# Edge stage of a GNN + MoE kernel: static order of GpSimd's gathers and scatters, own index semaphores, zeroing from SyncE's queue

## The chip, the cores and the metric

The kernel runs on one core of a Trainium2 chip (trn2). The metric is the device time of one execution in microseconds.

## The reference

Nodes N = 50000 with D = 256 features, 25000 edges, 8 experts. Cut to what matters:

```python
# stage 1: edges.  H in f16, w = edge_weight in f16
msgs = layernorm(x).astype(f16)[dst] * w[:, None]
x = x + segment_sum(msgs, src, num_segments=50000)      # f16 sums
# stages 2 and 3: a layer norm, a top-1 router over 8 experts with capacity, two-layer experts
h = layernorm(x)
idx, p = argmax/prob of softmax(h @ gate_w + gate_b)
x = x + (relu(h @ w1[idx] + b1[idx]) @ w2[idx] + b2[idx]) * (p * kept)
```

The change touches stage 1 alone.

## The kernel before, in words

The program has three stages, each a block of five engine programs with a barrier behind it: the edge stage (`edge_and_constants`), the router (`route_tokens`) and the experts (`run_experts`). The router reads what the edge stage added up in a DRAM buffer `agg`, so it starts only when the edge stage has ended on every engine.

The edge stage works in steps of 1024 edges: 25 steps, numbered 0 to 24, the last one overlapping the one before it. In each step:

- SyncE (SP) loads `dst_col`, `src_col`, `w_col` and `src_row` (src repeated on 128 partitions), lines 159 to 163. They share one semaphore `idx_loaded[h]` for each of `INPUTS` = 3 buffers, and wait until the step that used the buffer is computed (`edge_done`, line 157).
- GpSimd (POOL) gathers the rows of x that `dst` names: eight indirect transfers of 128 rows, `gather`, lines 186 to 198. It waits for all four loads of the step and for a free buffer of `rows`.
- VectorE takes the statistics of the rows once all eight have landed (line 305), builds comparison masks (line 292), scales the messages (line 340), and writes the `target` rows (line 349), which increments `edge_done`.
- ScalarE takes the square root, normalises (line 265), and copies TensorE's sums from PSUM to `sums` in four parts (line 275, `sums_out`).
- TensorE counts, and adds up the messages with equal src inside the step by 64 matmuls with the masks (lines 365 to 376).
- GpSimd scatters the sums into `agg` by eight indirect transfers that add (`scatter`, lines 200 to 215). Scatter s waits for `edge_done` and `sums_out` of step s and until scatter s-1 has landed, since two adds to one row must not overlap. Scatter 0 also waits until `agg` is zeroed.

`agg` is zeroed by 25 transfers of 1 MB, which ScalarE issues between its instructions of the first steps (`zero`, line 246). `sums` and `target` have `HOLD` = 6 buffers. GpSimd's order is written out by hand: gathers of steps 0 to 5, then in turn scatter s and gather s+6 (eight calls each) as long as there are steps, with a hardware loop in the middle (lines 217 to 238). The other engines run steps in order, unrolled by `HOLD`, with the first `HOLD` steps outside of the loop.

Of the kernel before, what the change touches and what calls it, by code (L numbers as in the profile page):

```python
# [27 lines left out]
I32 = mybir.dt.int32  # L28
# [28 lines left out]
HOLD = 6  # L57
INPUTS = 3
# [14 lines left out]
def edge_and_constants(nc, ctx, t):  # L73
# [22 lines left out]
    dst_col = sb("dst_col", [P, INPUTS, G], I32)  # L96
# [27 lines left out]
    agg_zeroed = sem("agg_zeroed")  # L124
    idx_loaded = [sem(f"idx_loaded{r}") for r in range(INPUTS)]
# [16 lines left out]
    AHEAD = HOLD - 1  # L142
# [6 lines left out]
    with nc.Block() as block:  # L149

        @block.sync
        def _(sp):
            def load(i, r):
                s, h = HOLD * i + r, r % INPUTS

                if not (isinstance(i, int) and s < INPUTS):
                    sp.wait_ge(edge_done, s + 1 - INPUTS)
                b = base_of(i, r)
                sp.dma_start(dst_col[:, h, :], row_view(dst[bass.ds(b, STEP)])).then_inc(idx_loaded[h], 16)
# [3 lines left out]
                    .then_inc(idx_loaded[h], 16)  # L163
            steps(sp, S, HOLD, load)

# [9 lines left out]
        def _(pool):  # L175
# [10 lines left out]
            def gather(i, r):  # L186
                s, h = HOLD * i + r, r % INPUTS

                pool.wait_ge(idx_loaded[h], 64 * (turn(i, r) + 1))
                pool.nop(nofuse=True)  # L190
                if not (isinstance(i, int) and s < INPUTS):
                    pool.wait_ge(edge_done, s + 1 - INPUTS)
                    pool.nop(nofuse=True)
                for c in range(G):
                    pool.indirect_dma_start(
                        out=rows[:, h, c, :], out_offset=None, in_=x[:, :],
                        in_offset=bass.IndirectOffsetOnAxis(ap=dst_col[:, h, c:c + 1], axis=0),
                    ).then_inc(gathered[h], 16)

            def scatter(i, r):  # L200
                s = HOLD * i + r
# [4 lines left out]
                if isinstance(i, int) and s == 0:  # L206
                    pool.wait_ge(agg_zeroed, 16 * ZEROS)
                else:
                    pool.wait_ge(added[r - 1], 16 * G * (i + 1 if r else i))
                    pool.nop(nofuse=True)  # L210
# [6 lines left out]
            for r in range(AHEAD):  # L217
                gather(0, r)
            gather(0, AHEAD)
            scatter(0, 0)  # L220
            for r in range(1, HOLD):
                gather(1, r - 1)
# [1019 lines left out]
```

## Time and profile before

| | us |
|---|---|
| median of 3 runs | 3526.37 |
| lowest and highest run | 3525.03, 3540.87 |
| the profiled execution's own time | 3569.06 |
| its span | 3567.3 |
| GpSimd's last call of the edge stage starts | 703.73 |
| the router stage's first instruction on GpSimd | 713.84 |

The profile comes from one execution, taken by the hardware profiler. Start times in the timeline are microseconds from the span's start. An entry "[12.13 <-DMA src_row]" says that the engine was idle for 12.13 us before the instruction and what ended that. "issue" is time in which the engine waited for nothing that the profile shows. POOL is GpSimd, DVE VectorE, ACT ScalarE, PE TensorE, SP SyncE, and a name with a q behind it is the engine's DMA issuing.

### The profile page before, as it was taken

How to read it: one execution, taken by the hardware profiler on the slowest of the kernel's cores; microseconds unless marked ns; L12 is line 12 of the kernel's file. 1: busy time of each engine (PE TensorE's matmuls, PEld its weight loads, DVE VectorE, ACT ScalarE, POOL GpSimd, SP SyncE). 2: the span in 40 equal slices, each digit the busy share in tenths (PEclk: the TensorE clock that was granted, in tenths of full speed). 3: DMA queues.
4: the chain of work that ended last, by engine and by line, in shares of the span. 5: the costliest groups of instructions: out<-in, count | busy, mean ns of one | idle time of the engine just before them, and what ended most of it. 6: DMA issues, size and time to landing. Idle time of an engine off the chain costs nothing.

```text
span 3567.3 us, 60077 instructions
## 1 busy us (share of the span) xinstructions
PE 2846.6 (80%) x18806; PEld 2603.9 (73%) x18807; DVE 2245.0 (63%) x5836; ACT 1539.7 (43%) x2638; POOL 1724.4 (48%) x1183
## 2 busy tenths in 40 slices
PE   4553434067677777499999999999999999999998
PEld 3443433067676667399898999888999989998987
DVE  5645555076566566377666677676677776667666
ACT  2322222044444444255444555454455545554443
POOL 4788887635555566333434333343433343334323
PEclk8666666555555555699999999999999999999999
DMA  8544444388787776311211211121211121111111
GB/s 313 153 89 77 87 78 86 29 269 252 249 259 248 228 240 207 115 48 56 66 57 44 72 48 52 49 67 57 67 48 47 56 67 47 48 51 49 42 47 37
DMA packets 306007, 374.74 MB, mean 105 GB/s; under 512 B 34887, under 2 KB 266340, under 8 KB 302608
## 3 DMA queue, kind: packets, MB, share of 16 engines
q1 hardware_dynamic: 224608, 202.49, 19.3%
q0 software_dynamic: 77728, 145.22, 14.9%
q10 hardware_dynamic: 3600, 26.22, 1.8%
q8 instruction: 28, 0.46, 0.1%
q14 instruction: 43, 0.35, 0.0%
HBM read 185.42 MB, written 196.46 MB: 107 GB/s over the span
## 4 chain that ended last, share of the span: by engine, by line
PE 53%; DVE 4%; issue 1%; DVEq 0%; DMA 0%; SPq 0%; ACT 0%; POOL 0%; POOLq 0%; ACTq 0%
PE u_Y L1181 27%; PE u_H L1170 23%; PE u_T L1153 3%; DVE y L1110 1%; DVE yo L1129 1%; DVE yo L1126 1%; DVE y L1115 0%; DVE hn L1078 0%; DVE low L1120 0%; DVE hlo L1098 0%; DVE yo L1124 0%; DMA slots<-blank 0%; DMA u_pay<-slots 0%; DVE scales L1073 0%; DVEq L1078 0%
## 5 line engine op out<-in xcount | busy, mean ns | idle before, releaser
L1010 POOL DMA_INDIRECT out_x<-yo,u_token x348 | 668.5, 1921 | 1261.4 <-DVE yo L1131 1179.5
L1181 PE MATMUL u_Y<-whi,hhi 128*128 128x256 f32 x2784 | 784.2, 282 | 1.5 <-DVE hlo L1098 1.5
L1181 PE MATMUL u_Y<-wlo,hhi 128*128 128x256 f32 x2784 | 775.4, 279 | 0.0
L1181 PE MATMUL u_Y<-whi,hlo 128*128 128x256 f32 x2784 | 774.8, 278 | 0.0
L1046 ACT ACTIVATE hm<-u_H,b1e 128x512 f32<-128x512 f32 (+1 forms) x736 | 487.9, 663 | 639.8 <-PE u_H L1170 627.0
L539 POOL DMA_INDIRECT slots<-pay,slot_i x392 | 415.3, 1059 | 325.5 <-DVE slot_i L748 210.3
L1170 PE MATMUL u_H<-xhi,whi 128*128 128x512 f32 (+1 forms) x1472 | 563.6, 383 | 8.0 <-issue 5.5
L1170 PE MATMUL u_H<-xhi,wlo 128*128 128x512 f32 (+1 forms) x1472 | 562.2, 382 | 0.0
L1170 PE MATMUL u_H<-xlo,whi 128*128 128x512 f32 (+1 forms) x1472 | 560.2, 381 | 0.0
L1181 PEld LDWEIGHTS u_Y<-whi,hhi 128*128 128x128 f32 x2784 | 528.4, 190 | 1.7 <-DVE hlo L1098 1.7
L1181 PEld LDWEIGHTS u_Y<-wlo,hhi 128*128 128x128 f32 x2784 | 528.8, 190 | 0.0
L1181 PEld LDWEIGHTS u_Y<-whi,hlo 128*128 128x128 f32 x2784 | 528.1, 190 | 0.0
L1110 DVE TENSOR_TENSOR y<-u_Y,b2e 128x256 f32<-128x256 f32 x348 | 123.9, 418 | 555.2 <-PE u_Y L1181 555.2
L1050 ACT ACTIVATE hhi<-hm 128x512 fp32r<-128x512 f32 (+1 forms) x736 | 448.7, 610 | 23.3
L1098 DVE TENSOR_TENSOR hlo<-hm,hhi 128x512 fp32r<-128x512 f32 (+1 forms) x736 | 454.0, 692 | 2.9 <-ACT hhi L1050 2.9
L604 PEld LDWEIGHTS ps_L<-gw,hT 128*128 128x128 f32 x1568 | 350.3, 332 | 43.9 <-ACT hT L566 26.5
L604 PE MATMUL ps_L<-gw,hT 128*128 128x8 f32 x1568 | 344.0, 353 | 39.8 <-ACT hT L566 24.5
L212 POOL DMA_INDIRECT agg<-sums,target x200 | 329.5, 1648 | 83.7 <-issue 58.8
L1170 PEld LDWEIGHTS u_H<-xhi,whi 128*128 128x128 f32 x1472 | 277.0, 188 | 64.8 <-issue 9.8
L1170 PEld LDWEIGHTS u_H<-xlo,whi 128*128 128x128 f32 x1472 | 277.2, 188 | 53.8
L1170 PEld LDWEIGHTS u_H<-xhi,wlo 128*128 128x128 f32 x1472 | 277.4, 188 | 50.4
L619 PE MATMUL ps_T<-ident,h 128*128 128x128 f32 x784 | 206.9, 430 | 115.0 <-ACT h L570 111.8
(137 smaller groups left out, 3747.9 us busy)
## 6 DMA issues: line engine op xcount, KB each, us to landing
xt<-in_x SPq DMA_DIRECT2D x49, 1024.0 KB
out_x<-pay SPq DMA_DIRECT2D x49, 1024.0 KB
u_pay<-slots SPq DMA_DIRECT2D x93, 534.0 KB, 3.8
agg<-zeros ACTq DMA_DIRECT2D x25, 1024.0 KB
at<-agg SPq DMA_DIRECT2D x49, 512.0 KB
raw<-in_L_ffn_w POOLq DMA_DIRECT2D x14, 1024.0 KB
src_row<-in_src SPq DMA_DIRECT2D x25, 512.0 KB
slots<-blank SPq DMA_DIRECT2D x8, 801.0 KB, 5.1
```

What stands on the lines that cost most here:

```text
L212: pool.indirect_dma_start(out=agg[:, :], out_offset=bass.IndirectOffsetOnAxis(ap=target[:, r, c:c + 1], axis=0), in_=sums[:, r, c, :], in_ ...
L539: pool.indirect_dma_start(out=slots[:, :], out_offset=bass.IndirectOffsetOnAxis(ap=slot_i[:, r, g:g + 1], axis=0), in_=pay[:, r, g, :], in ...
L604: last = pe.matmul(logits[:, g, :], hT[:, g * KD + kd, :], gw[:, kd, :], start=(kd == 0), stop=(kd == KD - 1))
L619: last = pe.transpose(ps_T[:, n, :], h[:, q, g, kd * P:(kd + 1) * P], ident[:])
L1010: pool.indirect_dma_start(out=out[:, :], out_offset=bass.IndirectOffsetOnAxis(ap=token[:, s:s + 1], axis=0), in_=yo[:, s, :], in_offset=No ...
L1046: act.activation(hm[:, f, cols], ps_H[:, f % 2, cols], ACT.Relu, bias=b1e[:, f:f + 1])\
L1050: act.activation(hhi[:, f, cols], hm[:, f, cols], ACT.Copy).then_inc(hhi_ready, 1)
L1098: v.tensor_tensor(hlo[:, f, cols], hm[:, f, cols], hhi[:, f, cols].bitcast(F32), ALU.subtract)\
L1110: last = v.tensor_tensor(y[:, s, :], ps_Y[:, s, 0:D], b2e[:], ALU.add)
L1153: last = pe.transpose(ps_T[:, k, s * P:(s + 1) * P], hn[:, s, k * P:(k + 1) * P], ident[:])
L1170: last = pe.matmul(ps_H[:, f % 2, cols], w1_at(w, buf, k, f), a[:, k, cols], start=(j == 0), stop=(j == len(passes) - 1))
L1181: last = pe.matmul(ps_Y[:, s, 0:D], a[:, f, rows], w2_at(w, buf, f), start=(f == 0 and j == 0), stop=(f == KF - 1 and j == 2))
```

## The change

- `HOLD` goes from 6 to 8, so `sums`, `target` and now `dst_col` have eight buffers; `INPUTS` from 3 to 4, so `rows`, `src_row`, `src_col` and `w_col` have four.
- `dst_col` gets semaphores of its own (`dst_loaded`). GpSimd waits for that load alone, VectorE for the other three. The load of `dst_col` is issued ahead of the wait for a free input buffer. The gather still waits until the step four before it is computed.
- The zeroing transfers move from ScalarE's to SyncE's queue: 13 behind the loads of step 3, and three each behind those of steps 4 to 7.
- GpSimd's program is static, without a hardware loop: all 64 gather calls of steps 0 to 7, scatter 0, and then the other 136 gather calls spread evenly, five or six of them ahead of each of the scatters 1 to 24.

```diff
--- before.py
+++ after.py
@@ -54,8 +54,8 @@
         return self.base + self.n
 
 
-HOLD = 6
-INPUTS = 3
+HOLD = 8
+INPUTS = 4
 
 
 def steps(eng, total, unroll, body):
@@ -93,7 +93,7 @@
     zeros = sb("zeros16", [P, 16 * D], F16)
     src_row = sb("src_row", [P, INPUTS, STEP], I32)
     src_col = sb("src_col", [P, INPUTS, G], I32)
-    dst_col = sb("dst_col", [P, INPUTS, G], I32)
+    dst_col = sb("dst_col", [P, HOLD, G], I32)
     w_col = sb("w_col", [P, INPUTS, G], F32)
     w16 = sb("w16", [P, 2, G], F16)
     w32 = sb("w32", [P, 2, G], F32)
@@ -122,6 +122,7 @@
     set_up = sem("set_up")
     pool_set = sem("pool_set")
     agg_zeroed = sem("agg_zeroed")
+    dst_loaded = [sem(f"dst_loaded{r}") for r in range(HOLD)]
     idx_loaded = [sem(f"idx_loaded{r}") for r in range(INPUTS)]
     gathered = [sem(f"gathered{r}") for r in range(INPUTS)]
     added = [sem(f"added{r}") for r in range(HOLD)]
@@ -139,7 +140,6 @@
 
     BANKS = G * D // 512
     PER_BANK = G // BANKS
-    AHEAD = HOLD - 1
     turn = lambda i, r: (HOLD // INPUTS) * i + r // INPUTS
     row_view = lambda ap: ap.rearrange("(p c) -> p c", c=G)
     agg_v = agg.rearrange("(p b r) d -> b p (r d)", p=P, r=16)
@@ -150,18 +150,32 @@
 
         @block.sync
         def _(sp):
+            def zero(count):
+                for _ in range(count):
+                    b = next(parts, None)
+                    if b is not None:
+                        sp.dma_start(agg_v[b], zeros[:]).then_inc(agg_zeroed, 16)
+
             def load(i, r):
                 s, h = HOLD * i + r, r % INPUTS
-
+                b = base_of(i, r)
+
+                sp.dma_start(dst_col[:, r, :], row_view(dst[bass.ds(b, STEP)])).then_inc(dst_loaded[r], 16)
                 if not (isinstance(i, int) and s < INPUTS):
                     sp.wait_ge(edge_done, s + 1 - INPUTS)
-                b = base_of(i, r)
-                sp.dma_start(dst_col[:, h, :], row_view(dst[bass.ds(b, STEP)])).then_inc(idx_loaded[h], 16)
                 sp.dma_start(src_col[:, h, :], row_view(src[bass.ds(b, STEP)])).then_inc(idx_loaded[h], 16)
                 sp.dma_start(w_col[:, h, :], row_view(weight[bass.ds(b, STEP)])).then_inc(idx_loaded[h], 16)
                 sp.dma_start(src_row[:, h, :], src[bass.ds(b, STEP)].partition_broadcast(P))\
                     .then_inc(idx_loaded[h], 16)
+                if isinstance(i, int) and i == 0 and r >= INPUTS - 1:
+
+                    if r == INPUTS - 1:
+                        sp.wait_ge(set_up, 1)
+                    zero(ZEROS - (HOLD - INPUTS) * 3 if r == INPUTS - 1 else 3)
+
+            parts = iter(range(ZEROS))
             steps(sp, S, HOLD, load)
+            assert next(parts, None) is None
 
             w1, w2, raw = t["w1"], t["w2"], t["raw"]
             WF = raw.shape[1] // 2
@@ -183,30 +197,30 @@
             pool.affine_select(out=ident[:], in_=ident[:], compare_op=ALU.not_equal, fill=1.0, base=0,
                                pattern=[[-1, P]], channel_multiplier=1).then_inc(pool_set, 1)
 
-            def gather(i, r):
-                s, h = HOLD * i + r, r % INPUTS
-
-                pool.wait_ge(idx_loaded[h], 64 * (turn(i, r) + 1))
-                pool.nop(nofuse=True)
-                if not (isinstance(i, int) and s < INPUTS):
-                    pool.wait_ge(edge_done, s + 1 - INPUTS)
+            def gather(s, c):
+                r, h = s % HOLD, s % INPUTS
+                if c == 0:
+                    pool.wait_ge(dst_loaded[r], 16 * (s // HOLD + 1))
                     pool.nop(nofuse=True)
-                for c in range(G):
-                    pool.indirect_dma_start(
-                        out=rows[:, h, c, :], out_offset=None, in_=x[:, :],
-                        in_offset=bass.IndirectOffsetOnAxis(ap=dst_col[:, h, c:c + 1], axis=0),
-                    ).then_inc(gathered[h], 16)
-
-            def scatter(i, r):
-                s = HOLD * i + r
+                    if s >= INPUTS:
+
+                        pool.wait_ge(edge_done, s + 1 - INPUTS)
+                        pool.nop(nofuse=True)
+                pool.indirect_dma_start(
+                    out=rows[:, h, c, :], out_offset=None, in_=x[:, :],
+                    in_offset=bass.IndirectOffsetOnAxis(ap=dst_col[:, r, c:c + 1], axis=0),
+                ).then_inc(gathered[h], 16)
+
+            def scatter(s):
+                r = s % HOLD
 
                 pool.wait_ge(edge_done, s + 1)
                 pool.wait_ge(sums_out, BANKS * (s + 1))
                 pool.nop(nofuse=True)
-                if isinstance(i, int) and s == 0:
+                if s == 0:
                     pool.wait_ge(agg_zeroed, 16 * ZEROS)
                 else:
-                    pool.wait_ge(added[r - 1], 16 * G * (i + 1 if r else i))
+                    pool.wait_ge(added[(s - 1) % HOLD], 16 * G * ((s - 1) // HOLD + 1))
                     pool.nop(nofuse=True)
                 for c in range(G):
                     pool.indirect_dma_start(
@@ -214,49 +228,28 @@
                         in_=sums[:, r, c, :], in_offset=None, compute_op=ALU.add,
                     ).then_inc(added[r], 16)
 
-            for r in range(AHEAD):
-                gather(0, r)
-            gather(0, AHEAD)
-            scatter(0, 0)
-            for r in range(1, HOLD):
-                gather(1, r - 1)
-                scatter(0, r)
-            with pool.Fori(1, S // HOLD - 1) as i:
-                gather(i, AHEAD)
-                scatter(i, 0)
-                for r in range(1, HOLD):
-                    gather(i + 1, r - 1)
-                    scatter(i, r)
-            n = S // HOLD - 1
-            gather(n, AHEAD)
-            scatter(n, 0)
-            gather(n + 1, 0)
-            for r in range(1, HOLD):
-                scatter(n, r)
-            scatter(n + 1, 0)
+            HEAD = HOLD * G
+            SPREAD = S * G - HEAD
+            for n in range(HEAD):
+                gather(n // G, n % G)
+            scatter(0)
+            for s in range(1, S):
+
+                for n in range(HEAD + SPREAD * (s - 1) // (S - 1), HEAD + SPREAD * s // (S - 1)):
+                    gather(n // G, n % G)
+                scatter(s)
             for r in range(HOLD):
-                pool.wait_ge(added[r], 16 * G * (n + (2 if r == 0 else 1)))
+                pool.wait_ge(added[r], 16 * G * (S // HOLD + (r < S % HOLD)))
 
         @block.scalar
         def _(act):
 
             act.wait_ge(set_up, 2)
-            parts = iter(range(ZEROS))
-
-            def zero(i, count=1):
-                for _ in range(count if isinstance(i, int) and i == 0 else 0):
-                    b = next(parts, None)
-                    if b is not None:
-                        act.dma_start(agg_v[b], zeros[:]).then_inc(agg_zeroed, 16)
-
-            zero(0, 2 + max(0, ZEROS - AHEAD * (BANKS + 2)))
 
             def body(i, r):
                 s, h, q = HOLD * i + r, r % 2, r % INPUTS
-                zero(i)
                 act.wait_ge(stats_ready, s + 1)
                 act.activation(std[:, h, :], mv[:, h, :, 1], ACT.Sqrt, bias=eps[:, 0:1]).then_inc(std_ready, 1)
-                zero(i)
 
                 act.wait_ge(scale_ready, s + 1)
                 if not (isinstance(i, int) and s < 2):
@@ -269,12 +262,10 @@
                 if not (isinstance(i, int) and i == 0):
                     act.wait_ge(added[r], 16 * G * i)
                 for b in range(BANKS):
-                    zero(i)
                     act.wait_ge(summed, BANKS * s + b + 1)
                     part = slice(b * PER_BANK, (b + 1) * PER_BANK)
                     act.activation(sums[:, r, part, :], ps_sum[:, part, :], ACT.Copy).then_inc(sums_out, 1)
             steps(act, S, HOLD, body)
-            assert next(parts, None) is None
 
         @block.vector
         def _(v):
@@ -296,7 +287,7 @@
             def body(i, r):
                 s, h, q = HOLD * i + r, r % 2, r % INPUTS
                 n = Count(s * PER + SET)
-                v.wait_ge(idx_loaded[q], 64 * (turn(i, r) + 1))
+                v.wait_ge(idx_loaded[q], 48 * (turn(i, r) + 1))
                 v.tensor_copy(srcf[:, h, :], src_col[:, q, :])
                 v.tensor_copy(w16[:, h, :], w_col[:, q, :]).then_inc(step, n.inc())
 
```

Two places show how instructions move. The first is GpSimd at the end of the edge stage. `rows<-in_x,dst_col` is a gather call, `agg<-sums,target` a scatter call; eight of either make a step. Before, the rows begin with the gather of step 23:

```order
L195 DMA rows<-in_x,dst_col 128x256 [waits idx_loaded2,edge_done]
L195 DMA rows<-in_x,dst_col 128x256 x7
L212 DMA agg<-sums,target 51200x256 [waits edge_done,sums_out,added5]
L212 DMA agg<-sums,target 51200x256 x7
L195 DMA rows<-in_x,dst_col 128x256 [waits idx_loaded0,edge_done]
L195 DMA rows<-in_x,dst_col 128x256 x7
L212 DMA agg<-sums,target 51200x256 [waits edge_done,sums_out,added0]
L212 DMA agg<-sums,target 51200x256 x7
L212 DMA agg<-sums,target 51200x256 [waits edge_done,sums_out,added1]
L212 DMA agg<-sums,target 51200x256 x7
L212 DMA agg<-sums,target 51200x256 [waits edge_done,sums_out,added2]
L212 DMA agg<-sums,target 51200x256 x7
```

In the kernel before, scatters 19 to 24 all follow the last gather; three of them are shown. After the change, the last twelve rows of the stage:

```order
L209 DMA rows<-in_x,dst_col 128x256 [waits dst_loaded7,edge_done]
L209 DMA rows<-in_x,dst_col 128x256 x3
L226 DMA agg<-sums,target 51200x256 [waits edge_done,sums_out,added5]
L226 DMA agg<-sums,target 51200x256 x7
L209 DMA rows<-in_x,dst_col 128x256 x4
L209 DMA rows<-in_x,dst_col 128x256 [waits dst_loaded0,edge_done]
L209 DMA rows<-in_x,dst_col 128x256
L226 DMA agg<-sums,target 51200x256 [waits edge_done,sums_out,added6]
L226 DMA agg<-sums,target 51200x256 x7
L209 DMA rows<-in_x,dst_col 128x256 x6
L226 DMA agg<-sums,target 51200x256 [waits edge_done,sums_out,added7]
L226 DMA agg<-sums,target 51200x256 x7
```

The gather call that waits for `dst_loaded7` is the first of step 23, the one that waits for `dst_loaded0` the first of step 24. The scatter behind `added5` is step 22, behind `added6` step 23, behind `added7` step 24. The last gather calls now stand just ahead of the last scatters.

The second place is the zeroing. Before, on ScalarE, at the start of the stage:

```order
L250 DMA agg<-zeros 128x4096 [waits set_up]
L250 DMA agg<-zeros 128x4096 x2
L258 ACT_TABLE_LOAD
L258 ACTIVATE e_std<-e_mv,eps 128x8 [waits e_stats_ready]
L250 DMA agg<-zeros 128x4096
L265 ACTIVATE norm<-rows,e_offset,e_rstd 128x256 [waits scale_ready]
L265 ACTIVATE norm<-rows,e_offset,e_rstd 128x256 x7
L250 DMA agg<-zeros 128x4096
L275 ACTIVATE sums<-ps_sum 128x512 [waits summed]
L250 DMA agg<-zeros 128x4096
L275 ACTIVATE sums<-ps_sum 128x512 [waits summed]
```

After the change, on SyncE, from the loads of step 3 to those of step 4:

```order
L163 DMA dst_col<-in_dst 128x8
L166 DMA src_col<-in_src 128x8
L167 DMA w_col<-in_edge_weight 128x8
L168 DMA src_row<-in_src 128x1024
L157 DMA agg<-zeros 128x4096 [waits set_up]
L157 DMA agg<-zeros 128x4096 x12
L163 DMA dst_col<-in_dst 128x8
L166 DMA src_col<-in_src 128x8 [waits edge_done]
L167 DMA w_col<-in_edge_weight 128x8
L168 DMA src_row<-in_src 128x1024
L157 DMA agg<-zeros 128x4096 x3
```

ScalarE issues no transfers any more, and SyncE has the 13 transfers between the loads of step 3 and `dst_col` of step 4.

## Rows read from the trace of the kernel before

**Rows 1.** The page, busy tenths of 40 slices of 89 us, and a DMA issue line.
```profile
POOL 4788887635555566333434333343433343334323
...
DMA  8544444388787776311211211121211121111111
...
agg<-zeros ACTq DMA_DIRECT2D x25, 1024.0 KB
```

**Rows 2.** Windows: us, busy PE, PEld, DVE, ACT, POOL, then PEclk, DMA share, GB/s.
```profile
50.00:60.00 10.00, 5.20 (x52) 4.48 (x53) 6.35 (x21) 4.04 (x8) 7.12 (x8) 0.54 1.01 418
254.00:274.00 20.00, 10.55 (x100) 9.69 (x100) 7.33 (x34) 2.11 (x4) 16.04 (x14) 0.76 0.48 99
```

**Rows 3.** Groups by line, 0 to 900 us, GpSimd's two calls.
```profile
L212 POOL DMA_INDIRECT agg<-sums,target x200 | 329.5, 1648 | 83.7 <-issue 58.8 <-DMA agg<-sums,target 12.6 <-DMA agg<-zeros 12.0
...
L195 POOL DMA_INDIRECT rows<-in_x,dst_col x200 | 194.3, 971 | 95.7 <-issue 61.9 <-DMA src_row<-in_src 33.5 <-DMA agg<-sums,target 0.3
```

**Rows 4.** Timeline of GpSimd, head: start us, duration us, instruction, [idle before].
```profile
7.94 1.14 POOL L195 DMA_INDIRECT rows<-in_x,dst_col  x1 [5.86 <-DMA src_row<-in_src]
...
16.91 0.95 POOL L195 DMA_INDIRECT rows<-in_x,dst_col  x1 [0.30 <-issue]
...
50.75 1.05 POOL L195 DMA_INDIRECT rows<-in_x,dst_col  x1 [12.13 <-DMA src_row<-in_src]
...
76.14 0.94 POOL L195 DMA_INDIRECT rows<-in_x,dst_col  x1 [15.53 <-DMA src_row<-in_src]
...
88.67 0.95 POOL L195 DMA_INDIRECT rows<-in_x,dst_col  x1 [2.46 <-issue]
...
111.31 1.63 POOL L212 DMA_INDIRECT agg<-sums,target  x1 [11.96 <-DMA agg<-zeros]
```

**Rows 5.** Timeline of GpSimd, the end of the stage.
```profile
603.34 0.94 POOL L195 DMA_INDIRECT rows<-in_x,dst_col  x1 [0.30 <-issue]
...
622.65 1.54 POOL L212 DMA_INDIRECT agg<-sums,target  x1 [2.54 <-DMA agg<-sums,target]
...
703.73 1.55 POOL L212 DMA_INDIRECT agg<-sums,target  x1 [0.30 <-issue]
713.84 0.13 POOL L525 IOTA token_i<- 128x8 int32 x1 [8.57 <-POOLq L149]
```

**Rows 6.** Timeline of ScalarE's queue, zeroing transfers.
```profile
3.27 2.17 ACTq L250 DMA_DIRECT2D agg<-zeros  x3
...
103.20 0.34 ACTq L250 DMA_DIRECT2D agg<-zeros  x1
```

**Rows 7.** Timeline of SyncE's queue, loads of steps 0, 3 and 4.
```profile
0.96 0.41 SPq L159 DMA_DIRECT2D dst_col<-in_dst  x1
...
41.74 0.33 SPq L159 DMA_DIRECT2D dst_col<-in_dst  x1
...
62.54 0.33 SPq L159 DMA_DIRECT2D dst_col<-in_dst  x1
```

**Rows 8.** Timeline of VectorE, head: statistics of step 0, targets of steps 0 and 3.
```profile
20.33 2.71 DVE L305 BATCH_NORM_STATS2 e_stats<-rows 128x6 f32<-128x256 f32 x8 [13.00 <-DMA rows<-in_x,dst_col]
...
41.55 0.17 DVE L349 TENSOR_TENSOR target<-shift,srcf 128x8 int32<-128x8 f32 x1
...
100.52 0.17 DVE L349 TENSOR_TENSOR target<-shift,srcf 128x8 int32<-128x8 f32 x1
```

**Rows 9.** Timeline of VectorE and ScalarE, step 24.
```profile
606.06 2.71 DVE L305 BATCH_NORM_STATS2 e_stats<-rows 128x6 f32<-128x256 f32 x8 [10.57 <-DMA rows<-in_x,dst_col]
...
620.92 0.17 DVE L349 TENSOR_TENSOR target<-shift,srcf 128x8 int32<-128x8 f32 x1
...
629.54 0.60 ACT L275 ACTIVATE sums<-ps_sum 128x512 f16<-128x512 f32 x1 [1.15 <-PE ps_sum L376]
```

**Rows 10.** Timeline of VectorE and ScalarE, step 10.
```profile
242.56 2.71 DVE L305 BATCH_NORM_STATS2 e_stats<-rows 128x6 f32<-128x256 f32 x8 [11.60 <-DMA rows<-in_x,dst_col]
...
273.68 0.60 ACT L275 ACTIVATE sums<-ps_sum 128x512 f16<-128x512 f32 x1 [5.90 <-remote]
```

## The prediction

> **What bounds the kernel now.** The page first: GpSimd (POOL) is the busiest engine of the first seventh of the span, at 7 to 8 tenths, and the DMA row falls from 8 tenths to 4 after the first slices [rows 1]. A stretch from the middle, 254 to 274 us, shows why nothing else bounds it: GpSimd is busy 16.0 of 20 us and in issue gaps for the rest, TensorE 10.6, VectorE 7.3, DMA at 0.48 [rows 2]. The groups by line over the first 900 us give the price of GpSimd's calls: 200 scatters of 1648 ns and 200 gathers of 971 ns, each with 0.30 us of issue ahead of it (58.8 and 61.9 us over some 195 calls) [rows 3]. So a gather call is 1.27 us, a scatter call 1.95 us, a step of eight and eight 25.8 us, and 25 steps 254 + 390 = 644 us.
>
> GpSimd's timeline gives the rest. The first gather starts at 7.9. Then come three waits for a step's index loads (12.1 and 15.5 us, and 2.5 at step 5), and one of 12.0 us for the zeroing of agg [rows 4]; at the end, where no gathers are left between scatters, five waits of 2.5 us for the scatter before to land [rows 5]. Check: 7.9 + 644 + (12.1 + 15.5 + 2.5 + 12.0 + 5 x 2.5 less 0.3 each in the issue already counted, 52) = 704; the last call ends at 703.73 + 1.55 = 705.3 [rows 5]. The next stage opens 8.6 us later and depends on that. A microsecond of the edge stage is a microsecond of the kernel.
>
> **Zeroing off ScalarE's queue.** The 25 issues cost ScalarE nothing it lacks (its copies wait for TensorE), so removing them: 0. What counts is when the 25 transfers of 1 MB land [rows 1].
>
> **The start.** GpSimd now waits for dst_col alone, not for src_row. The landing it waited for came at 7.9; dst_col is issued at 0.96 [rows 7], so the first gather comes about 4 us earlier. That gain reaches the end only if nothing waits behind it, and something does: rows has four buffers, so the gather of step g still waits for step g-4 to be computed. "Eight ahead" is eight gathered before the first scatter, not eight ahead of the computing. The first scatter (call its start T0) must wait for gather 7, which waits for the end of step 3. In the trace steps 0 and 3 end at 41.7 and 100.7 (DVE's target) [rows 8], about 20 us a step, against 10.2 us that eight gathers need. The computing sets the head, and I leave its pace as it is.
>
> Then gather 7 ends at 100.7 + 10.2 = 110.9. The last three zeroing transfers are issued behind the same end of step 3 and three loads, about 3 us after it; the last one before took 8.1 us from issue (103.2) to the scatter it released (111.3) [rows 4, 6]: 112. So T0 does not come earlier than the 111.3 of now, though 64 gathers stand before it and not 48. 13 of the zeroing transfers now come in one burst near 8 us (16 loads at 0.41 us and a little between them, from 0.96 [rows 7]). I add 3 us for it (bounds: 9 us below, if a head without scattered zeroing computes faster, to 15 above, the flood below). **T0 = 115.**
>
> **The middle.** After T0: 136 gathers x 1.27 = 172.7 and 200 scatters x 1.95 = 390.0. The 2.5 us landing waits go, covered by five or six gathers (6.3 us or more). Scatter calls are 1.54 us when VectorE is idle and 1.65 in the mean [rows 3, 5]; before, 160 of them lay beside VectorE's work of 20 steps, 21 us in all; now three of these steps are computed while GpSimd waits: -3 us. Steps 8 to 19 are gathered well ahead of their scatters: the last call of step 19 is followed by a whole scatter batch more than the next ones. Middle: 560 us.
>
> **The end, where the change pays.** The 136 calls are spread evenly over 24 gaps. The order shows what this does: the last call of step 24 is the call just before scatter 24; step 23's last call has two gathers behind it and then scatter 23; step 22's has four. A step needs all its eight calls before its statistics begin. Step 24 of the trace is such a step, computed with no gathers beside it: its last gather call ends at 604.28, the statistics start at 606.06, the target is written at 621.1, the last copy of its sums ends at 630.14 [rows 5, 9]: 25.9 us from the last gather to the release of its scatter. Before, this was hidden by five scatter batches. Now it is not:
> - scatter 24: 25.9 us of waiting,
> - scatter 23: 25.9 - 2 x 1.27 = 23.4,
> - scatter 22: 25.9 - 4 x 1.27 = 20.8,
> - scatters 21 and 20: steps whose last call is followed by one and three gathers, a scatter batch (15.6) and six gathers (7.6), so 24.5 and 27.0 us of cover. With gathers beside the copies a step takes longer: the one that starts its statistics at 242.56 ends its copies at 274.28, 31.7 us, against 24.1 in step 24 [rows 9, 10]. Between 1.4 us together and 11; I take 5.5.
>
> Sum of the waits: 75.6 us. The scatters form a chain, so each wait moves all that follows, and gathering and computing cannot run on meanwhile, since GpSimd issues both.
>
> **The sum**, in the profiled execution (span 3567.3, time 3569.06): GpSimd's last call ends at 115 + 560 + 75.6 = 750.6 against 705.3: **+45 us**. The profiled execution stands 43 us above the median of the three runs, 3526.37 (the highest of them is 3540.87); I take the difference over unchanged: 3526.4 + 45 = **3571 us**, 1.3% slower.
>
> **A page against the rows.** Index loads issued beside the zeroing took long: step 3's were issued from 41.7 and released GpSimd at 50.75, step 4's 62.5 and 76.1 [rows 4, 7]. They were on SP's queue while the zeroing was on ScalarE's. The Trainium skill, "DMA: Bandwidth & Descriptors", section "Queues, rings and completion order", says that SP and ACT own one ring each on the same 16 DMA engines, that an engine takes whole packets from the rings in turn, and consumes one ring in order. By that rule dst_col of step 4, now issued behind 13 transfers on one ring, waits for all of them, and each gather call waits for a packet of zeroing. The trace agrees that loads suffer; that they stand in line, no row here shows. My sum has 3 us for this, by that rule it has up to 15.
>
> **The rivals.**
> - *The flood sets the head.* One zeroing transfer is 1 MB, 64 KB per DMA engine, at the 418 GB/s of 50 to 60 us [rows 2] 2.5 us; a gather call is 128 KB, 0.3 us. If they alternate, a step's rows need 8 x 2.8 = 22 us to land and not 10. Step 0 is half issued before the burst and loses some 5 us, step 1 a few more. Step 4's indices come at 8.5 us + 13.6 MB / (418 less the gathers' 105 GB/s) = 52 us, and not at step 0's end at 42, which costs nothing, since gather 7 waits for step 3 anyway. If TensorE's first steps slow too, T0 is 130: +60, 3586 us. For it: DMA at 1.00 wherever zeroing runs. Against: step 0's last call ended at 17.9 and its statistics began at 20.3, 2.5 us later, with three such transfers issued ahead of it [rows 4, 6, 8].
> - *The waits at the end are halved.* If a step alone needs less than the trace's 25.9 us (VectorE has no earlier step to finish, TensorE no copies to wait for) the waits shrink threefold with each microsecond; at 15 us they are 15 + 12.5 + 9.9 = 37, the end is 115 + 560 + 37 = 712, +7: within 0.5%, 3533 us.
> - *The other side: no waits at the end.* The one mechanism is the cover. If spreading the calls kept computing ahead of scattering to the end, GpSimd would run without a pause, and the end would be 115 + 560 = 675: -30, 3496 us. It decides at a latency of 7.6 us (six gathers) for step 24 and less for the others. The start of the stage speaks for it, where three steps of gathers are in hand; step 24's 25.9 us [rows 9], of which the 9.0 us from the target to the last copy alone are more than the cover, speak against it.
> - *The change does nothing*: the head bound by computing, the end as before. But then scatter 24 would need its rows long before, and the order says otherwise.
>
> **How the numbers follow.** Forecast (three full waits, T0 106 to 122): 0.76. Flood on top: 0.11. Halved waits: 0.09. No waits: 0.04. Half a percent, 17.6 us, is about what a measurement of this kernel can tell from no change. Slower by more: forecast, flood and a little of the halved case, 0.88; within: 0.08; faster: 0.04. Range: below, T0 at 106, waits of 70 and scatters 10 us cheaper give +21; I go to +20, 3546. Above, the flood with 11 us at scatters 20 and 21 gives +66, 3592.
>
> **What the changed profile would show.** First gather near 4; step 3's end near 100; first scatter at 112 to 118, released by the zeroing or by the last gather's end; no waits for agg to land; then on GpSimd three waits of 20 to 26 us for ScalarE's copies before the last three scatter batches, and the last call near 750. TensorE's share in the later stages is unchanged. I am wrong if these three waits sum to under 50 us, or if T0 lies below 100 or over 130.

## The result and the profile after

The changed kernel takes 3586.96 us (median of four runs, 3579.25 to 3590.17). The kernel before takes 3533.62 us in four runs, the three of the table above among them. The ratio is 1.0148, 95% interval 1.0113 to 1.0184, and the medians lie 53 us apart, where 45 were forecast. 3586.96 lies inside the range of 3546 to 3592, 16 us above the 3571 that was said.

The page of the changed kernel, GpSimd and DMA in tenths of the 40 slices:

```profile
POOL 5688887426666666433433433343433343334323
...
DMA  8544444148888786321211211121211121111111
```

GpSimd is as busy as before up to the seventh slice and falls to 4 in the eighth (628 to 718 us), where it showed 6 [rows 1]; the router stage, visible as DMA at 8, fills the tenth slice and only half of the ninth. The waits of the edge stage, for GpSimd alone (engine, line, waited for: total us, times, longest):

```profile
POOL agg L226 <- ACT sums L267: 70.6, 3, 26.2
POOL rows L209 <- issue: 62.5, 196, 3.1
POOL agg L226 <- issue: 61.9, 193, 3.2
...
POOL rows L209 <- DVE target L340: 15.2, 2, 10.9
POOL rows L209 <- DMA dst_col<-in_dst: 14.5, 2, 13.1
...
POOL agg L226 <- DMA dst_col<-in_dst: 6.6, 1, 6.6
```

The first line is new: three waits of GpSimd for ScalarE's copies, 70.6 us. The landing waits (a scatter waiting until the scatter before it has landed in `agg`) are gone. A scatter waits for several semaphores, and the trace names one of them: scatter 0 does not wait for `dst_col` at all, and the 6.6 us in the last line are read here as its wait for the zeroing, which e2 below names at the same place. The groups of the two calls, against [rows 3]:

```profile
L226 POOL DMA_INDIRECT agg<-sums,target x200 | 324.3, 1621 | 140.0 <-ACT sums L267 70.6 <-issue 61.9 <-DMA dst_col<-in_dst 6.6
L209 POOL DMA_INDIRECT rows<-in_x,dst_col x200 | 197.2, 986 | 92.2 <-issue 62.5 <-DVE target L340 15.2 <-DMA dst_col<-in_dst 14.5
```

The calls cost nearly what they did, 27 ns less for a scatter, 15 ns more for a gather. GpSimd's timeline at the head, against [rows 4]:

```profile
3.53 1.14 POOL L209 DMA_INDIRECT rows<-in_x,dst_col  x1 [1.42 <-DMA dst_col<-in_dst]
...
57.39 0.95 POOL L209 DMA_INDIRECT rows<-in_x,dst_col  x1 [13.09 <-DMA dst_col<-in_dst]
...
106.37 0.94 POOL L209 DMA_INDIRECT rows<-in_x,dst_col  x1 [10.89 <-DVE target L340]
...
123.11 1.78 POOL L226 DMA_INDIRECT agg<-sums,target  x1 [6.64 <-DMA dst_col<-in_dst]
```

The gathers start 4.4 us earlier, gather 4 waits for its indices until 57, gather 7 for the end of step 3 until 106, and the first scatter comes at 123.1 (111.3 before). At the end, against [rows 5]:

```profile
605.29 1.61 POOL L226 DMA_INDIRECT agg<-sums,target  x1 [3.18 <-issue]
...
646.45 1.62 POOL L226 DMA_INDIRECT agg<-sums,target  x1 [20.24 <-ACT sums L267]
...
692.83 1.62 POOL L226 DMA_INDIRECT agg<-sums,target  x1 [24.14 <-ACT sums L267]
...
714.08 0.95 POOL L209 DMA_INDIRECT rows<-in_x,dst_col  x1 [0.30 <-issue]
...
741.24 1.61 POOL L226 DMA_INDIRECT agg<-sums,target  x1 [26.20 <-ACT sums L267]
...
754.28 1.54 POOL L226 DMA_INDIRECT agg<-sums,target  x1 [0.30 <-issue]
765.48 0.14 POOL L516 IOTA token_i<- 128x8 int32 x1 [9.66 <-POOLq L149]
```

These are scatters 21, 22, 23 and 24. Between the last gather call (714.08) and scatter 24 (741.24) stands step 24, alone:

```profile
716.82 2.71 DVE L296 BATCH_NORM_STATS2 e_stats<-rows 128x6 f32<-128x256 f32 x8 [34.56 <-DMA rows<-in_x,dst_col]
...
730.83 0.17 DVE L340 TENSOR_TENSOR target<-shift,srcf 128x8 int32<-128x8 f32 x1
...
739.78 0.60 ACT L267 ACTIVATE sums<-ps_sum 128x512 f16<-128x512 f32 x1 [1.15 <-PE ps_sum L367]
```

From the end of the last gather call, 715.03, to the end of the last copy, 740.38, is 25.3 us, against 25.9 in [rows 9]; the scatter starts 0.9 us after it. The last call ends at 755.8, 50.5 us later than before. The two profiled spans differ by 21 us only (3588.4 and 3567.3), since the router stage, from its first instruction on GpSimd to its last scatter call, took 741 us in the profiled execution before and 707 in this one. The first run below asks whether that is the change.

### The profile page after: what moved, and what is told of

Same layout as the page of the kernel before. It is cut to its first block, busy times and chain, and to the rows that moved or that the text cites. A ratio compares the mean times of both kernels' runs of the same rounds, so it can differ in the third digit from the quotient of the medians.

```text
span 3588.4 us, 59975 instructions
## 1 busy us (share of the span) xinstructions
PE 2837.7 (79%) x18806; PEld 2604.7 (73%) x18807; DVE 2245.5 (63%) x5836; ACT 1544.4 (43%) x2638; POOL 1733.7 (48%) x1183
## 4 chain that ended last, share of the span: by engine, by line
PE 53%; DVE 4%; issue 1%; DVEq 0%; DMA 0%; SPq 0%; ACT 0%; POOL 0%; POOLq 0%; ACTq 0%
PE u_Y L1172 27%; PE u_H L1161 24%; PE u_T L1144 3%; DVE y L1101 1%; DVE yo L1120 1%; DVE yo L1117 1%; DVE y L1106 0%; DVE hn L1069 0%; DVE low L1111 0%; DVE hlo L1089 0%; DVE yo L1115 0%; DMA slots<-blank 0%; DMA u_pay<-slots 0%; DVE scales L1064 0%; DVEq L1069 0%
## 5 line engine op out<-in xcount | busy, mean ns | idle before, releaser
L530 POOL DMA_INDIRECT slots<-pay,slot_i x392 | 424.9, 1084 | 282.3 <-DVE slot_i L739 166.7
L226 POOL DMA_INDIRECT agg<-sums,target x200 | 324.3, 1621 | 140.0 <-ACT sums L267 70.6
L357 PE MATMUL ps_cnt<-ones,earlier 128*128 128x1 f16 x200 | 31.4, 169 | 451.9 <-DVE earlier L325 405.0
L357 PEld LDWEIGHTS ps_cnt<-ones,earlier 128*128 128x128 f16 x200 | 25.2, 132 | 457.1 <-DVE earlier L325 410.4
```

The lines of the kernel that those rows point to most:

```text
L226: pool.indirect_dma_start(out=agg[:, :], out_offset=bass.IndirectOffsetOnAxis(ap=target[:, r, c:c + 1], axis=0), in_=sums[:, r, c, :], in_ ...
L357: last = pe.matmul(ps_cnt[:, c:c + 1], earlier[:, h, c, :], ones[:, 0:1], start=(c == 0), stop=True)
L530: pool.indirect_dma_start(out=slots[:, :], out_offset=bass.IndirectOffsetOnAxis(ap=slot_i[:, r, g:g + 1], axis=0), in_=pay[:, r, g, :], in ...
```

## Experiments

Each kernel ran beside the kernel before, on the same chip. Three chips were used, on which the kernel before takes 3567, 3441 and 3565 us; which chip the first comparison (3534 us) ran on is not on record. "First scatter" and "end" are the start of the first and the end of the last scatter call, in us of the profiled execution. "N gaps" says how many of the gaps between scatters got gather calls; the changed kernel has 24.

| run | ratio to before (95%) | first scatter | end |
|---|---|---|---|
| the changed kernel | 1.0148 (1.0113 to 1.0184) | 123.1 | 755.8 |
| e1, before again | one run, no ratio | 112.9 | 707.2 |
| e2, 22 gaps | 0.9944 (0.9929 to 0.9960) | 121.0 | 688.6 |
| e3, whole steps | 0.9984 (0.9971 to 0.9998) | 123.1 | 701.3 |
| e4, zeroing on ScalarE | 1.0160 (1.0141 to 1.0179) | 125.8 | 761.7 |
| b2, before, gather 24 late | 1.0076 (1.0062 to 1.0089) | 106.0 | 720.6 |
| b3, 22 gaps, seven steps ahead | 0.9941 (0.9928 to 0.9955) | 97.9 | 676.8 |
| e5, gather 3 held back | 1.0113 (1.0097 to 1.0128) | 104.8 | 739.4 |
| b4, b3 and e5 | 0.9934 (0.9920 to 0.9947) | 98.5 | 677.3 |
| c1, the changed kernel again | 1.0152 (1.0137 to 1.0168) | 124.4 | 757.7 |
| c2, 23 gaps | 0.9970 (0.9952 to 0.9988) | 124.2 | 698.5 |
| c3, b3 again | 0.9967 (0.9954 to 0.9980) | 112.4 | 690.7 |
| c4, six and three buffers, 22 gaps | 0.9951 (0.9934 to 0.9968) | 101.9 | 691.2 |

e1 to e4 ran on one chip, b2 to b4 and e5 on the second, c1 to c4 on the third.

**The kernel before again (e1).** No edit.

> The kernel before, unchanged, for a second profile. Theory A (the edge stage alone moved; the 21 us between the two profiled spans and the 53 us between the medians differ because the router stage of the first profile happened to be long, 741 us from its first instruction to its last scatter against 707 in the changed kernel): the edge stage again ends at 705 +- 3 us, the router stage takes 705 to 725, and the span is 3525 to 3545. Rival B (the changed edge stage makes the router stage 33 us shorter): the router stage again takes about 741 and the span is about 3567.

The edge stage ends at 707.2, as expected, the router stage takes 728 us and the span is 3555.7. For the router and the span neither theory's number came (705 to 725 or 741, and 3525 to 3545 or 3567). But in all profiled executions on this chip and the third, whichever kernel, the router stage takes 728 to 736, and on the second chip 616 to 619. So it goes with the chip and not with the edge stage, and Rival B is out. Why the first two profiles show 741 and 707 stays open: their chips are not on record. The edge stage's own 50 us is what the medians show.

**The end: 22 gaps (e2).**

```diff
-                for n in range(HEAD + SPREAD * (s - 1) // (S - 1), HEAD + SPREAD * s // (S - 1)):
+                for n in range(HEAD + SPREAD * min(s - 1, 22) // 22, HEAD + SPREAD * min(s, 22) // 22):
```

> The changed kernel with its 136 spread gather calls in the first 22 gaps and not in all 24, so that the last two scatters have no gathers ahead of them. Theory A (the three waits of 20, 24 and 26 us for step 22, 23 and 24 are the loss): they go, two landing waits of 2.2 us come, the first scatter stays near 123, the last call ends at 755.8 - 70.6 - 3 + 4.4 = 687 and the kernel is some 68 us faster than the changed one, 3519, about 15 us faster than before. Rival B (computing has become the bound of the last steps, as its steps come late): the waits move ahead to other scatters and less than half of the 70 us comes back, 3555 or more.

The end comes at 688.6, 687 was expected, and the kernel is 0.56% faster than before. GpSimd's idle times over 2 us from the first scatter on:

```profile
121.00 1.63 POOL L226 DMA_INDIRECT agg<-sums,target  x1 [4.89 <-DMA agg<-zeros]
```

```profile
657.24 1.54 POOL L226 DMA_INDIRECT agg<-sums,target  x1 [2.56 <-DMA agg<-sums,target]
...
674.16 1.54 POOL L226 DMA_INDIRECT agg<-sums,target  x1 [2.46 <-DMA agg<-sums,target]
```

All three waits for copies are gone, and nothing took their place but two landing waits. This one line of the change is the loss; the rest of it was worth a little.

How much, and by what, can be added up against e1, the kernel before on the same chip, which ends at 707.2. The first scatter comes 8.1 us later (121.0 for 112.9); 16 gather calls of 1.27 us more have been made by then, so 20.3 us fewer are left behind it; and two landing waits of 2.2 us stand where e1 has five, 6.6 us less. That gives 18.8 us, and 18.6 were measured.

**One gap fewer (c2).** The same edit with 23 for 22, on the third chip.

> The changed kernel with its 136 spread calls in 23 gaps: the last gather stands ahead of scatter 23, so one scatter batch covers step 24. Theory A (a wait is the latency of 25.5 us less what GpSimd issues after the step's last gather): one wait of 25.5 - 14.6 - 0.3 = 10.6 us ahead of scatter 24, at most 1 us ahead of scatter 23 (2 gathers, a scatter batch, 6 gathers: 25.2 us of cover), none ahead of 22; the last call 60 us before that of the changed kernel. Rival B (the steps at the end wait for each other on VectorE and ScalarE): waits of over 5 us ahead of scatters 22 and 23 stay.

```profile
660.28 1.62 POOL L226 DMA_INDIRECT agg<-sums,target  x1 [2.79 <-issue]
...
683.99 1.54 POOL L226 DMA_INDIRECT agg<-sums,target  x1 [8.36 <-issue]
```

Ahead of scatter 24 GpSimd waits 8.4 us (10.6 expected), ahead of 23 2.8 (up to 1), and the end is 59.2 us before that of c1 (60 expected). The two misses are one: step 23, with gather calls beside it, takes 25.9 us from its statistics to its last copy where step 24 takes 23.9, and what GpSimd waits ahead of scatter 23 covers step 24 as calls would. The trace names no cause for either wait ("issue"); that scatter 24 starts at 683.99, 0.8 us after the last copy ends at 683.18, shows what it waited for. With the waits of the changed kernel (20, 24 and 26 us at 24 gaps) and none at 22 the rule "latency less cover" holds within 2.2 us at four lengths of cover.

**The cause put into the kernel before (b2).**

```diff
-            gather(n + 1, 0)
             for r in range(1, HOLD):
                 scatter(n, r)
+            gather(n + 1, 0)
             scatter(n + 1, 0)
```

> The kernel before with one batch moved: the gather of step 24 stands between scatters 23 and 24 and not ahead of scatter 19. Theory A (a gather just ahead of its scatter exposes the step's whole latency, 25.9 us): GpSimd waits 25 to 26 us for ScalarE's copies ahead of scatter 24, scatter 19 gets a landing wait of 2.2 us and scatter 24 loses one; the last call ends at 706 + 26 = 732, ratio to before 1.007. Rival B (computing alone, with no gathers beside it and the clock up, is much shorter than the trace's step 24): the wait is 15 us or less, ratio 1.004 or less.

```profile
679.21 0.95 POOL L195 DMA_INDIRECT rows<-in_x,dst_col  x1 [0.30 <-issue]
...
705.96 1.62 POOL L212 DMA_INDIRECT agg<-sums,target  x1 [25.80 <-ACT sums L275]
```

One batch moved costs 25.8 us of waiting and 0.76% of 3441 us, 26 us. The end, 720.6, is not the 732 that was expected: on this chip the first scatter comes at 106.0 and not at 111.3, and the calls cost less. The wait and the ratio came as Theory A had them. So the late gather makes the wait, shown in both directions.

**Whole steps (e3).** As e2 with 17 for 22: eight calls ahead of scatters 1 to 17.

> The changed kernel with eight gather calls ahead of each of the scatters 1 to 17 and none later, as the kernel before orders them, but with eight steps ahead. Theory A (only the end's cover counts): seven bare scatters cost 7 landing waits of 2.2 us, 15 in all; the last call ends near 687 + 11 = 698, the kernel about 3530, level with before. Rival B (even spreading itself makes scatter and gather calls cheaper or the computing faster): 10 us or more worse than that, 3540 or more.

The end is 701.3 (698 expected), 12.7 us after e2's; seven landing waits of 2.2 us against two are 11 of it. The first scatter comes 2.1 us later as well. So spreading to scatter 22 is worth what the landing waits cost.

**The zeroing back on ScalarE (e4).** Three transfers at the start, then one between ScalarE's instructions, as before; all else as changed.

```diff
+            zero(0, 2)
...
+                zero(i)
                 act.wait_ge(stats_ready, s + 1)
```

> The changed kernel with the zeroing transfers back on ScalarE's queue, between its instructions as before; the late waits stay. Theory A (the burst of 13 transfers slows step 0, whose target came at 49.1 and not 41.7, and the index loads behind it): step 0's target comes at 42 again, step 3's at 100, the first scatter at 111 to 114 and not 123, the last call at 745, the kernel 8 to 12 us faster than the changed one, 3576. Rival B (the first scatter comes late because it stands behind 64 gathers, wherever the zeroing is issued): first scatter at 120 or later, kernel within 4 us of the changed one, 3587.

My expectation was wrong, and the numbers of Rival B came. Step 0's target comes at 49.0 again, the first scatter at 125.8, and the ratio is 1.016 where the changed kernel has 1.015. The burst is not what slows step 0. VectorE's target of step 0 in e4:

```profile
48.82 0.17 DVE L339 TENSOR_TENSOR target<-shift,srcf 128x8 int32<-128x8 f32 x1
```

What these kernels share is that GpSimd, with four row buffers, issues gather calls until 44 us, where three buffers stopped it at 38.6 and step 0 was done at 41.7. That gave a new theory: gather calls beside a step hold it up. Rival B's reason, the 64 gathers ahead, fits too for the first scatter, but says nothing of step 0.

**Gather 3 held back until step 0 is computed (e5), and the same on b3 (b4).**

```diff
-                    if s >= INPUTS:
+                    if s >= INPUTS - 1:
 
-                        pool.wait_ge(edge_done, s + 1 - INPUTS)
+                        pool.wait_ge(edge_done, max(1, s + 1 - INPUTS))
```

> The changed kernel with one wait more: gather 3 starts only when step 0 is computed, as with three input buffers. Theory A (gather calls beside a step hold up TensorE's counts and the copies: step 0's target came at 42 before and at 49 with gathers issued until 44, wherever the zeroing is issued): step 0's target comes at 41 to 43, step 3's at 98 to 101, the first scatter at 114 to 118 instead of 123, and the kernel is 5 to 8 us faster than the changed one, ratio to before 1.013. Rival B (DMA at full load from the burst of zeroing is what holds up step 0): its target still comes at 47 to 49 and nothing is gained.

> b3 with the pause of e5. Theory A: first scatter 5 to 7 us before b3's, last call near 672, ratio to before 0.990. Rival B (the pause moves step 0's end only, and the zeroing sets the first scatter): within 2 us of b3.

This told nothing of the theory, since the runs fell on the second chip: step 0's target comes at 34.0 with the pause (e5) and at 34.6 without (b3), where gathers run until 45. From its statistics to its target step 0 takes 14 us there in either, and 14.0 in b2; before, it took 21.4 [rows 8]. None of the times expected for e5 fits that chip, and b4 ends within 0.5 us of b3, as its Rival B had it. e5 still has its three waits at the end, 20.7, 24.4 and 26.3 us, so the loss is there on the second chip too. Its ratio, 0.9934, is the best one measured, but its interval overlaps b3's.

**Seven steps ahead and the zeroing one load earlier (b3, again as c3).** With e2's gaps:

```diff
-            HEAD = HOLD * G
+            HEAD = (HOLD - 1) * G
...
-                    zero(ZEROS - (HOLD - INPUTS) * 3 if r == INPUTS - 1 else 3)
+                    zero(ZEROS - 9 if r == INPUTS - 1 else 3)
```

> The kernel with 22 gaps (e2) and, besides, seven steps gathered ahead of the first scatter and not eight, and the zeroing issued one load earlier (16, 3, 3, 3 behind the loads of steps 3 to 6). Theory A (the first scatter waits for the end of step 3 through gather 7 and the last zeroing): its time falls from 121 to about 100, the eight calls of step 7 follow later (10 us), the last call ends near 678 and not 688.6, the kernel is about 10 us faster than e2, ratio to before 0.9915. Rival B (what GpSimd gains at the first scatter it waits out later, since computing sets the pace until step 8): the last call ends within 3 us of e2's.

> b3 again (22 gaps, seven steps ahead, zeroing one load earlier), beside the changed kernel on one chip. Theory A: ratio to before 0.991 to 0.995; against the changed kernel 75 to 80 us less in the last call. Rival B (its gain came from one chip's fast first steps): where the first steps are slow the first scatter comes at 110 or later and the ratio is 0.997 or more.

On the second chip the first scatter comes at 97.9, as expected, but the kernel before gains there too (its first scatter, in b2, is at 106.0), and the ratio is 0.9941, not 0.9915. On the third the first scatter comes at 112.4 and the ratio is 0.9967, near Rival B's numbers; the last call comes 67 us before that of the changed kernel on this chip, and 75 to 80 were expected. The end, 690.7, is no earlier than e2's 688.6, since the eight calls that were not made ahead are made later: what an earlier first scatter gains, fewer calls ahead of it give back.

**The changed kernel again (c1).** No edit.

> The changed kernel again, on one chip with the next three. Theory A (the end waits are the loss on every chip, the start's part depends on how fast the chip computes the first steps): waits of 20, 24 and 26 us ahead of scatters 22 to 24; ratio to before 1.011 to 1.017. Rival B (the loss of the first comparison was of one chip): ratio under 1.008.

Waits of 20.8, 22.8 and 25.5 us, ratio 1.0152: the first comparison repeats on a chip where the kernel before takes 3565 us.

**Six and three buffers (c4).** e2's gaps, with the buffers of the kernel before:

```diff
-HOLD = 8
-INPUTS = 4
+HOLD = 6
+INPUTS = 3
```

> The changed kernel with HOLD = 6 and INPUTS = 3, as many buffers as before, and 22 gaps: static order and own index semaphores alone, six steps ahead. Theory A (more buffers bring nothing, the order does): first scatter at 97 to 105, no waits for computing at the end, last call within 4 us of b3's, ratio to before 0.991 to 0.995. Rival B (three row buffers stall the spread gathers): GpSimd waits for VectorE's target between scatters, last call 10 us or more later than b3's.

The end is 691.2 against 690.7 of c3 on the same chip, and the ratio 0.9951, at the edge of what was expected. So the added buffers bring nothing that shows. Where its gain over the kernel before comes from can again be added up, against e1 (on another chip; no profile of the kernel before was taken on this one): the same 48 calls are made ahead, the first scatter comes 11.0 us earlier (101.9 for 112.9), and three landing waits fewer are worth 6.6 us; 17.6 us in all, and the ends differ by 16.0. The larger part is the earlier first scatter: the last zeroing transfers are issued at 86.9 from SyncE's queue, where e1 issues its last one at 105.2 between ScalarE's instructions. No run moved the zeroing alone with six and three buffers.

c4 also bears on what e5 left open. On one chip, target of step 0, first c1 (four row buffers, gathers until 44.6), then c4 (three, gather 3 waits for this step, so the calls stop at 34.2):

```profile
49.34 0.17 DVE L340 TENSOR_TENSOR target<-shift,srcf 128x8 int32<-128x8 f32 x1
```

```profile
39.20 0.17 DVE L340 TENSOR_TENSOR target<-shift,srcf 128x8 int32<-128x8 f32 x1
```

10 us earlier, though 16 zeroing transfers and not 13 are issued in the burst beside it. The other reading would be that DMA at full load holds the step up. The stretch from 36 to 44 us, first of e4 (gather calls going on, the zeroing spread out), then of c4 (no gather calls, the burst), speaks against it (columns: busy PE, PEld, DVE, ACT, POOL, granted clock, DMA share, GB/s):

```profile
36.00:44.00 8.00, 1.96 (x36) 1.87 (x34) 0.35 (x2) 0.00 (x0) 6.17 (x7) 1.00 0.37 107
```

```profile
36.00:44.00 8.00, 7.18 (x64) 6.25 (x65) 5.72 (x27) 0.60 (x1) 0.00 (x0) 1.00 1.02 426
```

At a DMA share of 0.37 TensorE is busy for 2.0 of 8 us beside the gather calls, and at 1.02 for 7.2 us without them; the granted clock is 1.00 in both. In the changed kernel TensorE's adding up of step 0 starts at 48.44, after 6.96 us idle, and the gather calls had ended at 44.30; in the kernel before the two times are 41.15 (where it runs on without gaps) and 38.62. That speaks for the gather calls and against the zeroing. How they hold up the other engines is not shown, and an edit of nothing but the gather's wait on such a chip was not run.

## Why the prediction was right, and where it was off

- **The waits at the end.** Forecast: 25.9, 23.4, 20.8 us, and 5.5 for scatters 20 and 21, 75.6 in all. Measured: 26.2, 24.1, 20.2, and 3.0 (0.46 and 3.18, less the usual issue gap), 72.7 with the gaps taken off. The mechanism and the places were right, and so were the sizes of the three large waits. For scatters 20 and 21 the low end of "1.4 to 11" was the better one; where the 11 came from the prediction does not say. e2, c2 and b2 show the cause by taking it away, by giving part of the cover back, and by putting it in elsewhere.
- **The first scatter.** 115 was said, 106 to 122 allowed, and 123.1 came: the one clear error. The sum was 112 for the last zeroing (issued about 3 us after step 3, then 8.1 us) and 3 for the burst. Two of its terms were off. Step 3 ended at 105.6 and not at 100.7, so the last three transfers were issued at 108.0, 4.3 us later than 103.7. Here "the computing sets the head, and I leave its pace as it is" did not hold, since four row buffers let gather calls run on beside step 0, and on these chips that goes with a later step 0 (49.1 for 41.7). And from that issue to the first scatter it took 15.1 us and not 8.1, 7.0 us more. The 8.1 us were read from a single transfer, while three are issued together here; c1, e2, c2, c3 and c4, which issue three as well, show 13.6 to 14.9 us. 4.3 and 7.0, less the 3 allowed for the burst, are 8.3 us, against the 8.1 by which the sum was off. By e4 those 3 us had the wrong reason.
- **The middle.** 560 us was said, and 755.8 - 123.1 - 72.7 = 560.0. That it fits so closely is luck: scatters came 27 ns cheaper, 5.4 us in all where 3 were allowed, and gathers 15 ns dearer, 2 us.
- **The sum.** The edge stage came out +50.5 for +45, the medians +53 for +45. The 8.1 us of the first scatter, less the 2.9 that the waits came out shorter, are the 5.2 of the edge stage; in part the two errors cancelled.
- **Carrying it over to the median.** I took the profiled execution's +43 us over the median as a constant. It was not one: the changed kernel's profiled execution lies within 4 us of its median. 34 of the 43 us lie in the router stage, 741 us against 707. 3569 us is what a chip like those of e1 and c1 gives for the kernel before (3567 and 3565), so the profile may have come from another chip than the three runs; the record does not say. It did no harm to the forecast difference.
- **The page's rule.** dst_col of step 4 was issued at 27.35 behind the 13 transfers and released GpSimd at 57.39; 52 was worked out. By the Trainium skill, "DMA: Bandwidth & Descriptors", section "Queues, rings and completion order", one ring is consumed in order, and the trace agrees: the wait of 13.1 us at gather 4 names this load. In e4, with the zeroing on ScalarE's queue, gather 4 starts at 49.8, as soon as step 0 is computed (49.0). The late load cost the changed kernel nothing, as was said, because gather 7 waits for step 3 anyway.
- **The rivals.** The flood (T0 at 130) did not come in full, but it was nearer than the forecast's words suggest. At a DMA share of 1.02 from 12 to 50 us step 0's rows were used at 19.8, 6.4 us after its last gather call had ended (13.46), where before it was 2.5 us. So all but 0.5 of the 4.4 us by which the gathers started earlier were lost; the rival had said "some 5 us" for step 0. The burst on SyncE's queue is not needed for that: e4, with three transfers ahead, has 20.46 after 13.45. The halved waits fell with the 25.3 us of step 24. The kernel without waits fell with it too; its threshold of 7.6 us was misread, since no call at all stands between the last gather and scatter 24.

## What to carry to other kernels

Where one in-order engine issues both the inputs and the outputs of a pipeline, price the end of its order by itself: the wait ahead of the last output is the latency of a step less what the engine issues between that step's last input and its output. Spreading input calls evenly to the last output empties the pipeline just there; ending the spread two outputs early turned +1.5% into -0.6%. More lead at the start is worth the calls that it moves out of the busy stretch, less what it delays the first output: here 20.3 less 8.1 us in e2, and no more than six buffers brought in c4.

## What the runs showed of the hardware

**The chips differ in how soon an engine goes on after another.** In the profiled execution before, ScalarE's copies waited 213.9 us in the edge stage for something that the trace calls "remote", with the matmuls that they depend on recorded as ended; on the second chip (b2) no such wait stands in the list. In e1, on a chip where the kernel before takes 3567 us, it is 233.9 us. The waits of the kernel before:

```profile
ACT sums L275 <- remote: 213.9, 39, 12.2
DVE shift L343 <- remote: 23.6, 5, 8.0
```

In the kernel before, once the scatters have begun, a step beside gather calls takes 30 to 33 us from its statistics to its last copy (before and e1; [rows 10] is one), and 24.1 in step 24, which has none beside it. On the second chip (b2) every such step takes 23 to 24 us, with gather calls or without. The router stage shows it too. From 800 to 1300 us of the kernel before (e1) and of b2, whose router stage is the same (columns as above):

```profile
800.00:1300.00 500.00, 374.77 (x1970) 356.11 (x1970) 310.82 (x1246) 226.35 (x448) 297.91 (x276) 0.50 0.81 251
```

```profile
800.00:1300.00 500.00, 442.35 (x2364) 426.26 (x2364) 369.37 (x1482) 273.63 (x541) 387.67 (x332) 0.50 0.96 299
```

The granted clock is 0.50 in both (1.2 GHz), and the second chip does a fifth more in the same time. What is behind "remote" stays open. The waits at the end are nearly the same on all of them (70.6 us in the changed kernel, 69.1 in c1, 71.4 in e5); the head is not, which is why a change to it should be timed on more than one.
